# Four groups of dummy matmuls left out of layers 0 and 2 of a four-layer kernel

## The reference

```python
def _layernorm(x, axis=-1, eps=1e-05):
    m = jnp.mean(x, axis=axis, keepdims=True)
    v = jnp.var(x, axis=axis, keepdims=True)
    return (x - m) / jnp.sqrt(v + eps)
...
# layer 2, attention: 16 heads of 8
q = proj(Wq, bq); k = proj(Wk, bk); v = proj(Wv, bv)
scores = jnp.einsum('bhqd,bhkd->bhqk', q, k) / scale
scores = jnp.where(causal[None, None], -jnp.inf, scores)
attn = jax.nn.softmax(scores, axis=-1)
out = jnp.einsum('bhqk,bhkd->bhqd', attn, v)
return out @ Wo.T + bo
...
# layer 2, feed forward: each token goes to one of 8 experts, 512 tokens each
logits = x @ w_switch + b_switch
probs = jax.nn.softmax(logits, axis=-1)
routes = probs.argmax(axis=-1)
oh = (routes[:, None] == jnp.arange(E)[None, :]).astype(jnp.int32)
pos = (jnp.cumsum(oh, axis=0) * oh).sum(-1) - 1
```

## Time and profile before

| what | value |
|---|---|
| median of 3 runs | 2823.55 us (2822.97 to 2823.79) |
| profiled execution | 2830.87 us, span 2829.6 us |
| mean granted clock of PE | 0.945 of full speed |
| busy: PE, DVE, ACT, POOL | 83%, 73%, 50%, 30% of the span |
| matmuls on PE, recorded | 18123 |

### The profile page before, as it was taken

How to read it: one execution, slowest core, us unless ns; L and a number is a source line. 1 busy time by engine, 2 the same in 40 slices (tenths; PEclk the granted TensorE clock), 3 DMA queues, 4 the chain that set the end, 5 groups by cost and what they waited for, 6 DMA issues and landing times.

```text
span 2829.6 us, 47422 instructions
## 1 busy us (share of the span) xinstructions
PE 2360.7 (83%) x18123; PEld 1711.4 (60%) x18265; DVE 2056.6 (73%) x4405; ACT 1408.4 (50%) x3592; POOL 852.2 (30%) x459
## 2 busy tenths in 40 slices
PE   4788888988988787888888888868888877888886
PEld 2466666666655574666666666645555555666665
DVE  3489999999988645676776767645666633888987
ACT  0355555555555215676767676613334333454553
POOL 0044344344444402222222222210000001554553
PEclk9899999999999888999999999969999997988998
DMA  1010110111110460000000000000100002454553
GB/s 65 16 46 31 46 46 31 46 39 39 46 45 32 160 220 1 1 1 1 1 1 1 1 1 1 1 22 23 30 24 12 8 20 68 170 184 151 175 169 118
DMA packets 71346, 148.23 MB, mean 52 GB/s; under 512 B 6864, under 2 KB 37072, under 8 KB 70608
## 3 DMA queue, kind: packets, MB, share of 16 engines
q1 hardware_dynamic: 69072, 140.99, 14.9%
q0 software_dynamic: 2048, 4.20, 0.4%
HBM read 135.46 MB, written 9.18 MB: 51 GB/s over the span
## 4 chain that ended last, share of the span: by engine, by line
PE 55%; DVE 23%; ACT 13%; issue 7%; DMA 0%; POOL 0%; another core or an unknown queue 0%; SPq 0%; DVEq 0%; ACTq 0%
PE psum L861 4%; PE psum L679 4%; DVE h L1536 3%; PE psum L727 3%; PE psum L566 3%; PE psum L486 3%; PE psum L675 3%; PE psum L320 3%; ACT pr L1879 3%; PE psum L397 3%; DVE h L1527 3%; DVE mx L1413 2%; ACT dA L1831 2%; PE psum L686 2%; ACT pt L1923 2%
## 5 line engine op out<-in xcount | busy, mean ns | idle before, releaser
L2137 POOL TENSOR_TENSOR h<-h,Crep 128x1024 f32<-128x1024 f32 x128 | 371.7, 2915 | 597.4 <-DVE h L1536 597.4
L2119 POOL TENSOR_TENSOR pr<-pr,rsum 128x512 f32<-128x512 f32 x192 | 220.5, 1161 | 588.7 <-DVE rsum L1379 588.7
L1413 DVE TENSOR_REDUCE mx<-psum 128x4 f32<-128x1024 f32 (+1 forms) x192 | 229.2, 1217 | 116.5 <-PE psum L684 116.5
L1536 DVE TENSOR_TENSOR_SCAN h<-dA,h 128x1024 f32<-128x1024 f32 x128 | 291.8, 2302 | 3.9 <-DVE h L1527 0.5
L861 PE MATMUL psum<-h,pack_wf 128*128 128x256 f32 x1024 | 246.9, 397 | 4.0 <-POOL h L2137 4.0
L1923 ACT ACTIVATE pt<-psum 128x1024 f32<-128x1024 f32 x192 | 186.8, 1016 | 121.9 <-PE psum L686 121.9
L2171 POOL TENSOR_TENSOR h<-h,Crep 128x1024 f32<-128x1024 f32 x64 | 179.7, 2808 | 219.7 <-DVE h L1304 219.4
L861 PEld LDWEIGHTS psum<-h,pack_wf 128*128 128x128 f32 x1024 | 202.2, 201 | 34.5 <-POOL h L2137 5.2
L1879 ACT ACTIVATE pr<-psum,nb 128x256 f32<-128x256 f32 (+1 forms) x512 | 211.9, 437 | 13.7 <-DVE nb L1371 13.7
L2020 ACT ACTIVATE dA<-delta,A 128x255 f32<-128x255 f32 x512 | 211.4, 494 | 13.1 <-DVE h L1536 11.7
L1889 ACT ACTIVATE prT<-psum 128x512 f32<-128x512 f32 x192 | 116.6, 607 | 132.7 <-PE psum L580 132.0
(11 more groups left out here) (340 smaller groups left out, 5258.8 us busy)
## 6 DMA issues: line engine op xcount, KB each, us to landing
Crep<-c_rows SPq DMA_DIRECT2D x64, 512.0 KB, 3.8
Brep<-bc_rows SPq DMA_DIRECT2D x64, 512.0 KB, 3.9
Crep<-bc_rows SPq DMA_DIRECT2D x64, 512.0 KB, 6.3
w1r<-m_w SPq DMA_DIRECT2D x32, 256.0 KB, 6.3
w2r<-m_w SPq DMA_DIRECT2D x32, 256.0 KB
pack_wf<-wf SPq DMA_DIRECT2D x1, 3192.0 KB, 11.4
slots<-zero SPq DMA_DIRECT2D x12, 256.0 KB, 6.8
w1s<-s_w SPq DMA_DIRECT2D x8, 256.0 KB, 2.8
```

The source lines that it names most:

```text
L1413: ve.e.tensor_reduce(mx[:, qb, 2 * h:2 * h + 2, groups[0]:groups[-1] + 1], k.psum[:, base:base + 2, :].rearrange("p i (n x) -> p i n x", n ...
L1536: ve.e.tensor_tensor_scan(flat(h), flat(k.dA[c][g % 2]), flat(h), 0.0, ALU.mult, ALU.add).then_inc(*k.set("scanned", 0, b, g, c))
L2119: po.e.tensor_tensor(p3, p3, bcast(k.rsum[n][:, 0:len(heads[r])], P * (q + 1), 2), ALU.mult).then_inc(*k.set("normed", 1, b, p, r))
L2137: po.e.tensor_tensor(h[:, :, :], h[:, :, :], k.Crep[n % 3][:, :, :], ALU.mult).then_inc(*k.set("hC", 0, b, g, c))
```

## The change

The calls of `pe_idle` in `pe_pre0`, `pe_quad`, `pe_max_turn` and `pe_pv` are taken out; those in `pe_results` and `pe_ffn` stay. No result depends on them.

```diff
@@ pe_pre0
     bk = pe_take(k, 0)
-    pe_idle(k, bk, 2)
     pe.wait_ge(*k.at("gv", b))
@@ pe_quad
     if c == 0 and kind == "keys":
-        if l:
-            pe_idle(k, banks[0], 7)
         pe.wait_ge(*k.at(f"negmax{b % 2}", l, b))
@@ pe_max_turn
     pe.wait_ge(*k.at(*k.slot_read[s]))
-    if l:
-        pe_idle(k, k.bank[2 * s], 6)
     pe.wait_ge(*k.at("mx", l, b, 2, 1))
@@ pe_pv
-    if l == 0 and half == 0:
-        pe_idle(k, bk, 4)
     pe.wait_ge(*k.at("exp", l, b, c, 1))
```

## The result

The changed kernel is slower: its time over the kernel before's, on the same chip, is 1.0061 (95% interval 1.0042 to 1.0081). The median of its five runs is 2840.37 us (2836.11 to 2847.94), against 2823.55 us for five runs of the kernel before (2820.19 to 2828.74). The forecast was 2822.5 us, and its range ended at 2836: the time is outside. Of the rivals, the second (the clock becomes the bound, 2838 us) came nearest in time, though the loss is in another layer than the one it leaned on.

A forecast was written before the change was run, and what follows sets the result against it. Layer 0 has DVE nearly full (93%); layer 2 is set by a round trip PE, DVE, ACT, PE. Terms -3.0 - 1.0 + 0 + 2.0 + 1.0 = -1.0 us, applied to 2823.55, gave 2822.5 us, range 2811 to 2836.

The forecast's parts named there:

- the clock term of layer 0: Layer 0: two more turns of 16 with a low-clock stretch at 1.0 us each, +2.0 us (0 to +8).
- rival 2: Clock becomes the bound: falls bring on more falls in layers 0 and 2; +14.5 us, 2838 us, chance 0.28.
- The term for the two at the gates: Layer 0, gates' values: a 1.45 us wait for ACT's exponential swallows the two dummies, so 0 gain.
- The four at the values: Layer 0's values: DVE's own work covers the 0.9 us less on PE, so about 0 gain.
- Layer 2, turned maxima: Transposes behind the six dummies start earlier: 0.2 us a turn over 15 turns, -3.0 us (0 to -4.4).
- Layer 2, keys' scores: Seven dummies ahead of the keys' matmuls: ACT ends at the same instant, so 0 (ends 0 and -6.2 us).
- the test "25.7 us or less": Sign that the keys' scores forecast is wrong: a turn of layer 2 takes 25.7 us or less.
- Layer 2, start: Thirteen dummies in layer 2's first turn: up to 2.5 us gained, less slower clock rise; -1.0 us (-2.5 to +2).
- Layer 2, clock: Low-clock stretches in five of layer 2's 15 turns at 0.2 us each, +1.0 us (0 to +10).
- the mark of 0.93: Sign that the clock forecast is wrong: layer 0's granted clock under 0.93.
- Rival 1: Dummies were on the path: keys' scores and layer 2's start gain in full; -11 us, 2812.5 us, chance 0.28.
- Rival 3: Clock stays at 1.00 everywhere, no falls: -4.0 us, 2819.5 us, chance 0.15.

The follow-up runs named there:

- experiment 6: Kernel before with both of layer 0's dummy groups left out and 4 dummies more ahead of the results' matmuls; ratio 1.0067.
- experiment 7: Kernel before with layer 0's dummies left out except in the start (2 for sequences 0 to 2, 4 for sequence 0); ratio 1.0071.
- 10: Kernel before with layer 2's dummies, from sequence 1 on, cut to 4 at the turned maxima and none at the keys' scores; ratio 0.9978.
- 8: Kernel before with layer 2's two dummy groups left out except for sequence 0; ratio 0.9980.

## Why the prediction was wrong

**The step that failed** is the clock term of layer 0, "two more such turns of 16", at "a low stretch costs 1.0 us there". Both factors were too small. Eight of the eleven inner turns hold a low stretch, four of them two. Against 53.2 us the first low stretch costs 1.6 and both together 2.6, so 4 x 1.6 + 4 x 2.6 = 16.8 us (14.5 against the eleven turns of before, which had one fall of 1.0 and 53.3 for 53.2; the other 1.8 of the 16.3 us are in the turns at both ends), where the term had 2.0 and its upper end 8 x 1.0 = 8. The number eight was in rival 2; the price came from one turn, whose stretch fell on state sums later in the turn. I took a price from the one place where it had been seen, and not from the place where the edit opened a hole: the matmuls behind it, L720 to L359, feed a copy of DVE that waits for PE even at the high clock, 0.70 us. The term was reasoned from PE's busy time in a turn (47.19 to 45.9 us), and experiment 6 shows that this does not decide the clock.

**The term for the two at the gates** ("a wait of 1.45 us [...] swallows them") is true of their time and false of their worth. They were free and held the clock. This is the same error, seen from the other side: two dummies in front of a hole were costed as PE time alone. The four at the values, costed at 0, gain 0.13 us a turn when they go, and the kernel loses it again in the layer's last two turns (787.3 against 787.4 us in all).

**A term that was missing** is the start of layer 0, 6.8 us in the profile. I had one for the start of layer 2 only. Its size stays open (experiment 7).

**Layer 2, turned maxima:** right. Predicted 0.2 us a turn, measured 0.23 (with the seven gone), and the transposes wait for the last maximum.

**Layer 2, keys' scores:** predicted 0, measured 0.51 us a turn, 6.6 us over thirteen; the end of -6.2 and the test "25.7 us or less" had it. The row named PE as the releaser of the exponential, with 0.41 us of idle time. I set that aside because ACT's own L1722 ended at the same instant as the scores. But ACT's end explains no idle time behind it, and the kernel after shows that ACT does not even wait for that end: once PE is early, the exponential starts 0.11 us after the start of L1715, where it had been 0.61 us. The difference of 0.50 us is the 0.51 of a turn.

**Layer 2, start:** the forecast was -1.0 us; the first two turns took 56.9 us and before 56.0, +0.9, within the ends of the term (-2.5 and +2) but of the other sign; kernels with layer 2 untouched have 53.0 to 56.1, so the runs do not tell. **Layer 2, clock:** forecast +1.0 us, five turns at 0.2; thirteen turns took 335.9 us where 13 x 25.50 is 331.5, so +4.4. Of these, five turns with a low stretch are 1.8, about 0.35 each, so this term was near; 2.6 is the turn with the late DMA. The layer as a whole gained 4.2 us where the sum for it said -3.0.

**The rivals.** Rival 2 had the right sign, the right cause in the clock and nearly the right time (2838), but the time partly by luck: its sum was 8 us of falls in layer 0 and 10.5 in layer 2. Layer 2 keeps a clock of 0.97 and gains; it was layer 0 whose clock came down to the mark of 0.93. Nor do the runs show its mechanism, falls that bring on the next: in the five kernels with falls behind the hole, a turn with two low stretches is always followed by one without any. Whether a turn's first stretch brings on its second is open. Rival 1's mechanism was right for layer 2 and was outweighed. Rival 3, the clock stays at 1.00, is refuted. It was the outcome by the Trainium skill's rule ("TensorE: Matmul & The Clock Gate", "Why this matters for your kernels"), that it is long gaps between bursts of matmuls that bring the throughput down. In the steady turns of layer 0 the longest gap of PE is 1.89 us, and the clock fell right behind it in eight of them; the trace does not agree with the rule, and the measurement decides.

## What to carry to other kernels

Work that nobody reads can still be useful: before leaving it out, ask of each piece separately what it costs (is it hidden by the wait behind it?) and what it holds up (is there a hole behind it, and which matmuls run next, with whom waiting for them?). Price a clock fall at the place where it will happen, by what stands there at its length under the low clock and by who waits for it, not by a fall seen elsewhere in the turn. Decide for each group by itself: keeping layer 0's and dropping layer 2's gave the gain of 0.26%, and keeping as many in layer 2 as the wait hides (10) took away the low stretches but no time that the runs could show.

## What the runs showed of the hardware

- A turn's busy share did not decide the granted clock: at 88% of PE busy it was 0.97 in one kernel and 1.00 in another. Two dummies of 0.22 us at the right place made a difference of 12 us over fifteen turns.
- The low stretches come in a fixed pattern: in the change the turns soon repeat 53.2, 54.8, 55.8 us every third turn; with only the two out, 53.3 and 56.0 alternate from the sixth on. Why three and two was not tried.
- An activation can start before the recorded end of the one ahead of it: L1916 starts 0.11 us after L1715, which takes 0.20 us. An end on ACT that coincides with another event is no proof that ACT was the limit.
- The DMA that writes the maxima was late once in the steady part of layer 2, in the same turn (the eighth) in all seven kernels in which the seven dummies do not cover it: PE's wait was 1.1 to 1.7 us, where it is otherwise about 0.37. It lengthened the turn by 0.9 to 2.6 us in five of them. In 8 and 10, where the clock stayed at 1.00 in that turn and the wait was under 1.2 us, it cost nothing. In experiment 6, which has all of layer 2's dummies, the same turn is 26.99 instead of 26.25 us. Which transfer it met is open.
- Executions of the same code differ by some 3 us at the start of layer 2 (53.0 to 56.1 us for the first two turns) and by as much or more at the start of layer 0; effects there under that size need more than one profile.
